# A transformer block on one core: another order of the global attention's pair with three probability buffers, and weights split per stage with finer waits in the layers

## The chip, the cores and the metric

The kernel runs on one core of a Trainium2 chip. The metric is device time in microseconds (us). A core has TensorE (PE in the profile, its weight loads PEld), VectorE (DVE), ScalarE (ACT), GpSimd (POOL) and SyncE (SP), which here only issues DMAs. Each engine runs its own instructions strictly in the order written; they meet through semaphores.

## The reference

The input is four batches of 1024 tokens of 256 numbers. Cut to what matters:

```
h = layernorm(x) * (1 + ca) + sa
q, k, v = tanh(h @ W + b)                      # 16 heads of 64, causal
x = x + ga * tanh(softmax(q k^T / 8) v @ Wo + bo)
h = layernorm(x) * (1 + cb) + sb
for l in range(2):                             # the layers, on h
    q, k, v = shift_token(h) @ wqkv[l]         # 8 heads of 64; norms, scales and rotary on q and k
    h = h + local_attention(q, k, v) @ wo[l]   # own window of 128 and the one before
    a, g = layernorm(shift_token(h)) @ w1[l] + b1[l]
    h = h + (a * gelu(g)) @ w2[l] + b2[l]
x = x + gb * h
```

`shift_token` takes the second half of the features from the token before.

## The kernel before

Matrix products of full precision are made of three: both factors are split into a high part, rounded by a copy or an activation, and a low part, the difference (`three_products`: high by high, high by low, low by high).

**Global attention** (`phase_attention`). Heads are worked in pairs, eight pairs in each of four batches, so 32 rounds of one body that is written out twice (`par` 0 and 1). A pair has twelve units (`UNITS`): a block of 512 queries against 128 keys, the first block with four units on the diagonal (512, 384, 256 and 128 queries), the second with four full ones and four on the diagonal. For a unit PE makes scores (`scores`), ACT the exponential (`probs`), DVE a high copy `p_hi` and a low part `p_lo`, and PE the products with the values (`value_products`, 24 matmuls for a full unit). In the same pair the projections of the next pair are made (`project`, six of them, named in `PROJ`: two for values, then queries and keys). ACT takes each tanh twice, once in full and once rounded, and DVE makes the low part (`split_projection`). The values are transposed by `values`. After units 3 and 11 the sums are divided out (`normalise`, one buffer `ctx_tok`), transposed (`context`) and split (`high_context`, `low_context`). `split_weights` prepares the projection weights of the pair after next. Scores, probabilities and their two parts have two buffers each; a loop over units puts the products of unit u behind the scores of u + 2, and `PROJ_AT`, `VALUES_AT` and `CTX_AT` say at which unit the other steps stand. After eight pairs comes the output projection of the batch.

**Layers** (`phase_layers`). The stream x, 32 tiles of 128 tokens, stays in SBUF. A layer has a body per tile (projection, rotary, local attention, output projection, added to x by DVE's L1314), and then a feed-forward part of eight chunks of four tiles. The weights of both come into one tile `raw` and are split into one pair `w_hi`, `w_lo`: before the first tile for the projection (ACT L998, DVE L1151), and again between the tiles and the chunks for the feed-forward part. SP copies x one token further into `shifted`, batch by batch as the tiles end (L898, L899). DVE waits for all four batches before the statistics of chunk 0 (`chunk_statistics`), then come Pool's power (L946), the normalisation (L1244), PE's transposes (L1432), ACT's and DVE's parts and the projections:

```
                    split_weights(4 * l + 2, F_COLS, 0)
                    hold(dve, s["tick"], (s["shift_in"], 128 * l + 128))
                    chunk_statistics(l, 0, 0, 0)
```

In a tile Pool makes the inverse norms (L936, L937), adds the rotary halves (L941), stages a tile of x (L928) and carries the last token over (L923, L925). In a chunk it adds the bias b2 to x (L974) and makes a power.

Semaphores that DVE, ACT, POOL and PE raise start at 4; `at(n)` adds it. `hold` waits for semaphores and then raises a counter that nobody waits for.

## Time and profile before

| what | value |
|---|---|
| runs | 2948.11 us median of 3 (2948.1 to 2950.08) |
| profiled execution | 2949.01 us, span 2947.2 us |
| busy, share of the span | PE 86%, DVE 70%, ACT 54%, POOL 18% |
| global attention, first scores to the last pair | 111 to 1147 us |
| first projection of layer 0 | 1231 us |
| tiles of layer 0 / chunks of layer 0 | 1262 to 1813 us / 1856 to 2072 us |
| first projection of layer 1 | 2079 us |

The span is what the profiler saw of the program; the profiled execution's time has 1.8 us around it. Busy shares are means over stages with different limits. A line number is one of the code above.

### The profile page before, as it was taken

How to read it: one execution, taken by the hardware profiler on the slowest of the kernel's cores; microseconds unless marked ns; L12 is line 12 of the kernel's file. 1: busy time of each engine (PE TensorE's matmuls, PEld its weight loads, DVE VectorE, ACT ScalarE, POOL GpSimd, SP SyncE). 2: the span in 40 equal slices, each digit the busy share in tenths (PEclk: the TensorE clock that was granted, in tenths of full speed). 3: DMA queues.
4: the chain of work that ended last, by engine and by line, in shares of the span. 5: the costliest groups of instructions: out<-in, count | busy, mean ns of one | idle time of the engine just before them, and what ended most of it. 6: DMA issues, size and time to landing. Idle time of an engine off the chain costs nothing. (4 is left out here: it accounts for less than half of the span.)

```text
span 2947.2 us, 65973 instructions
## 1 busy us (share of the span) xinstructions
PE 2541.4 (86%) x21520; PEld 1928.2 (65%) x21520; DVE 2056.4 (70%) x4571; ACT 1586.2 (54%) x3034; POOL 528.7 (18%) x534
## 2 busy tenths in 40 slices
PE   5699989989998998199999995899799999994996
PEld 3466656666666666177777774788577777773885
DVE  5588778858885885667777774566567777773656
ACT  2577567646764674356656654333466565652332
POOL 0000000000000000333343342111233433431111
PEclk7899999999999999599999998899899999996998
DMA  4400020010002000400000000100100000000003
GB/s 148 154 11 16 6 73 12 15 65 12 16 11 69 11 16 17 146 1 0 7 2 5 4 3 7 45 0 0 34 0 7 0 7 0 7 0 7 0 0 114
DMA packets 74545, 77.25 MB, mean 26 GB/s; under 512 B 4224, under 2 KB 67320, under 8 KB 72952
## 3 DMA queue, kind: packets, MB, share of 16 engines
q1 hardware_dynamic: 74488, 76.46, 7.9%
q8 instruction: 40, 0.66, 0.1%
q14 instruction: 17, 0.14, 0.0%
HBM read 55.48 MB, written 16.78 MB: 25 GB/s over the span
## 5 line engine op out<-in xcount | busy, mean ns | idle before, releaser
L502 ACT ACTIVATE at_p<-at_ps_s,at_shift 128x1024 f32<-128x1024 f32 (+3 forms) x384 | 342.9, 901 | 91.6 <-PE at_ps_s L561 39.9
L434 DVE TENSOR_TENSOR at_p_lo<-at_p,at_p_hi 128x1024 f16<-128x1024 f32 (+3 forms) x384 | 367.9, 958 | 12.1
L1023 ACT ACTIVATE ly_probs<-ly_masked,ly_small,ly_rq 128x256 f32<-128x256 f32 x512 | 302.3, 592 | 63.9 <-DVE ly_small L1206 63.2
L74 PE MATMUL ly_ps<-ly_w_hi,ly_operands 128*128 128x512 f32 (+1 forms) x792 | 293.7, 371 | 15.6 <-DVE ly_operands L1156 9.0
L429 DVE CAST at_p_hi<-at_p 128x1024 f16<-128x1024 f32 (+3 forms) x384 | 213.8, 557 | 94.8 <-PE at_ps_o L575 52.6
L75 PE MATMUL ly_ps<-ly_w_lo,ly_operands 128*128 128x512 f32 (+1 forms) x792 | 273.4, 345 | 0.0
L76 PE MATMUL ly_ps<-ly_w_hi,ly_operands 128*128 128x512 f32 (+1 forms) x792 | 273.1, 345 | 0.0
L573 PE MATMUL at_ps_o<-at_v,at_p_hi 128*128 128x65 f16 x2304 | 248.9, 194 | 24.3 <-DVE at_p_lo L434 24.3
L1409 PEld LDWEIGHTS ly_ps<-ly_values,ly_probs_T 128*128 128x128 f32 x2048 | 258.9, 192 | 15.6 <-issue 0.4
L573 PEld LDWEIGHTS at_ps_o<-at_v,at_p_hi 128*128 128x128 f16 x2304 | 209.9, 96 | 85.1 <-DVE at_p_lo L434 44.3
L1409 PE MATMUL ly_ps<-ly_values,ly_probs_T 128*128 x2048 | 260.1, 270 | 0.0
L574 PE MATMUL at_ps_o<-at_v,at_p_hi 128*128 128x64 f16 x2304 | 247.3, 194 | 0.0
L575 PE MATMUL at_ps_o<-at_v,at_p_lo 128*128 128x65 f16 x2304 | 245.7, 192 | 0.0
L1032 ACT ACTIVATE ly_probs_T<-ly_ps 128x512 f32<-128x512 f32 x256 | 150.3, 587 | 167.1 <-PE ly_ps L1409 150.1
L1389 PE MATMUL ly_ps<-ly_operands_plain 64*128 64x256 f32 x1040 | 183.7, 430 | 50.9 <-DVE ly_small L1203 50.9
L74 PE MATMUL at_ps_m<-at_hT,at_w_hi 128*128 (+1 forms) x396 | 177.0, 447 | 57.2 <-DVE at_v L395 37.2
L1203 DVE CUSTOM_DVE_ANT_0 ly_masked<-ly_ps,ly_mask 128x256 f32<-128x256 f32 x520 | 198.4, 419 | 25.4 <-DVE ly_mask L1303 11.7
L575 PEld LDWEIGHTS at_ps_o<-at_v,at_p_lo 128*128 128x128 f16 x2304 | 213.5, 99 | 0.0
L574 PEld LDWEIGHTS at_ps_o<-at_v,at_p_hi 128*128 128x128 f16 x2304 | 213.1, 97 | 0.4
L1055 ACT ACTIVATE ly_probs<-ly_ps,ly_b 128x512 f32<-128x512 f32 x96 | 66.3, 690 | 256.1 <-PE ly_ps L76 256.1
L471 ACT ACTIVATE at_stage<-at_ps_m,at_bias 128x512 f32<-128x512 f32 x198 | 136.1, 687 | 118.0 <-PE at_ps_m L76 100.4
L905 POOL MEMSET ly_expo<- 128x8 f32 x1 | 0.1, 104 | 1095.3 <-POOLq L331 1095.3
(209 smaller groups left out, 6343.9 us busy)
## 6 DMA issues: line engine op xcount, KB each, us to landing
at_hT<-hT_hi SPq DMA_DIRECT2D x5, 1024.0 KB, 5.2
at_hT<-hT_lo SPq DMA_DIRECT2D x5, 1024.0 KB, 7.7
at_w_raw<-in_Wv SPq DMA_DIRECT2D x34, 128.0 KB, 2.1
at_w_raw<-in_Wq SPq DMA_DIRECT2D x34, 128.0 KB, 2.3
at_w_raw<-in_Wk SPq DMA_DIRECT2D x34, 128.0 KB, 2.3
n_x<-in_states SPq DMA_DIRECT2D x4, 1024.0 KB, 11.6
hT_hi<-n_hi SPq DMA_DIRECT2D x8, 512.0 KB, 3.0
hT_lo<-n_lo SPq DMA_DIRECT2D x8, 512.0 KB, 3.1
```

Of the source, the lines that this page charges most:

```text
L74: pe.matmul(out, w_hi, x_hi, start=first, stop=False, skip_group_check=True)
L75: pe.matmul(out, w_hi, x_lo, start=False, stop=False, skip_group_check=True)
L76: return pe.matmul(out, w_lo, x_hi, start=False, stop=last, skip_group_check=True)
L429: dve.tensor_copy(p_hi[u % 2][:, :, off:], probs[u % 2][:, :, off:]).then_inc(p_hi_done, 1)
L434: dve.tensor_tensor(p_lo[u % 2][:, :, off:], probs[u % 2][:, :, off:], p_hi[u % 2][:, :, off:], ALU.subtract).then_inc(p_lo_done, 1)
L502: step = act.activation(probs[u % 2][:, :, off:], ps_s[u % 2][:, :, off:], ACT.Exp, bias=shift[:], scale=SCORE_SCALE)
L573: pe.matmul(out, ph, ones_hi, start=(kt == 0 and t == 0), stop=False, skip_group_check=True)
L574: pe.matmul(out[:, 0:DH], ph, lo, start=False, stop=False, skip_group_check=True)
L575: step = pe.matmul(out, pl, ones_hi, start=False, stop=(kt == qc * CT + t), skip_group_check=True)
L1023: step = act.activation(pr[:, j % 2, h, :], sm[:, j % 2, h, :], ACT.Exp, bias=small[:, j % 2, 1, h:h + 1], scale=rq[:, par, 2 * j + h:2 * ...
L1203: dve.tensor_tensor_reduce(sm[:, j % 2, h, :], ps_s[h][:, 0:2 * P], mask[:, par].rearrange("p a b -> p (a b)"), 1.0, -3.0e38, ALU.add, ALU ...
L1409: step = pe.matmul(ps_pv[:, cols], pT[:, (2 * slot + h) * P:(2 * slot + h + 1) * P], vv[:, v_slots[slot], cols], start=(j == 0 and h == 0 ...
```

## The change

In the global attention the loop over units and its tables give way to an order written out for PE, ACT and DVE. Probabilities and their parts have three buffers. Values' products, projections and contexts stand at other places; both contexts now come at the end of the pair, and ACT's weight split stands behind tanh 4. In the layers the attention's and the feed-forward part's weights have tiles of their own; the low part lies over the raw weights. The split for the feed-forward part is made by Pool, a piece in each tile, and the split for the next layer's attention by Pool, a piece in each chunk; so are the rotary tables, after the last chunk. Wo is loaded straight to its place. DVE waits for the shifted copy of a batch when it needs it, and SP waits for a batch's copy before it issues the next. In the last layer the preparation for a next one is made too and not used.

```diff
-LAG = 2
...
-PROJ_AT = {1: 0, 2: 1, 6: 2, 7: 3, 9: 4, 10: 5}
-VALUES_AT = {3: 0, 4: 1}
-CTX_AT = 11
...
+P_RING = 3
+NQKV_FREE = (NPJ - 1, NPJ)
...
+        probs = [a.sb(f"at_p{i}", [P, 2, CH]) for i in range(P_RING)]
+        p_hi = [a.sb(f"at_p_hi{i}", [P, 2, CH], F16) for i in range(P_RING)]
+        p_lo = [a.sb(f"at_p_lo{i}", [P, 2, CH], F16) for i in range(P_RING)]
...
+                def high_probs(it, u):
+                    off = unit_offset(u)
+                    dve.wait_ge(exp_done, at(it * NU + u + 1))
+                    dve.wait_ge(pv_done, at(it * NU + u + 1 - P_RING))
...
+                def reciprocals(it, c):
+                    dve.wait_ge(pv_done, at(it * NU + (CT, NU)[c]))
...
+                def normalise(it, c):
+                    n = it * NC + c
                     dve.wait_ge(r_done, at(n + 1))
+                    if c == 1:
+                        dve.wait_ge(ct_mm, n)
...
-                            normalise(it * NC + 1, it * NU + NU)
+                            ahead, dst = NPJ * (it + 1), 1 - par
+                            high_probs(it, 0)
+                            low_probs(it, 0)
+                            high_probs(it, 1)
+                            high_probs(it, 2)
+                            low_probs(it, 1)
+                            low_probs(it, 2)
+                            split_projection(ahead, 0, dst)
+                            split_projection(ahead, 1, dst)
+                            high_probs(it, 3)
+                            low_probs(it, 3)
+                            high_probs(it, 4)
+                            low_values(it + 1, dst)
+                            reciprocals(it, 0)
+                            low_probs(it, 4)
+                            normalise(it, 0)
+                            high_probs(it, 5)
+                            high_probs(it, 6)
+                            low_probs(it, 5)
+                            low_probs(it, 6)
+                            high_probs(it, 7)
+                            low_probs(it, 7)
+                            high_probs(it, 8)
+                            low_probs(it, 8)
+                            split_projection(ahead, 2, dst)
+                            high_probs(it, 9)
+                            high_probs(it, 10)
+                            low_probs(it, 9)
+                            low_probs(it, 10)
+                            high_probs(it, 11)
+                            low_probs(it, 11)
+                            split_projection(ahead, 3, dst)
+                            split_projection(ahead, 4, dst)
+                            reciprocals(it, 1)
+                            normalise(it, 1)
                             split_weights(it + 2)
+                            low_context(it * NC, hp, 0)
+                            split_projection(ahead, 5, dst)
                             low_context(it * NC + 1, hp, 1)
...
@@ -464,11 +497,20 @@
                     hold(act, tick, (ld_w, 48 * n + 48), (pj_mm, at(NPJ * n)))
                     act.activation(w_hi[:], w_raw[:], ACT.Copy).then_inc(wh_done, 1)
...
+                def exps(it, u):
+                    off = unit_offset(u)
+                    act.wait_ge(sc_done, it * NU + u + 1)
+                    act.wait_ge(p_lo_done, at(it * NU + u + 1 - P_RING))
+                    act.activation(probs[u % P_RING][:, :, off:], ps_s[u % 2][:, :, off:], ACT.Exp,
+                                   bias=shift[:], scale=SCORE_SCALE).then_inc(exp_done, 1)
...
+                def tanh_full(base, i, hp):
...
+                def tanh_hi(base, i, hp, dst):
...
+                            ahead, then, dst = NPJ * (it + 1), (hp + 1) % HP, 1 - par
+                            exps(it, 0)
+                            exps(it, 1)
+                            tanh_full(ahead, 0, then)
+                            exps(it, 2)
+                            tanh_hi(ahead, 0, then, dst)
+                            exps(it, 3)
+                            tanh_full(ahead, 1, then)
+                            tanh_hi(ahead, 1, then, dst)
+                            exps(it, 4)
+                            exps(it, 5)
+                            exps(it, 6)
+                            high_values(it + 1, dst)
+                            tanh_full(ahead, 2, then)
+                            tanh_hi(ahead, 2, then, dst)
+                            exps(it, 7)
+                            tanh_full(ahead, 3, then)
+                            exps(it, 8)
+                            exps(it, 9)
+                            tanh_hi(ahead, 3, then, dst)
+                            exps(it, 10)
+                            tanh_full(ahead, 4, then)
+                            exps(it, 11)
+                            tanh_hi(ahead, 4, then, dst)
+                            split_weights(it + 2)
+                            tanh_full(ahead, 5, then)
+                            tanh_hi(ahead, 5, then, dst)
+                            high_context(it * NC, hp, 0)
                             high_context(it * NC + 1, hp, 1)
...
+                            buf = ((it + 1) // HP) % 2
+                            ahead = NPJ * (it + 1)
+                            scores(b, it, par, 1)
+                            project(it, 0, buf)
+                            scores(b, it, par, 2)
+                            scores(b, it, par, 3)
+                            project(it, 1, buf)
+                            value_products(b, it, par, 0)
+                            scores(b, it, par, 4)
+                            scores(b, it, par, 5)
+                            values(0, ahead)
+                            value_products(b, it, par, 1)
+                            values(1, ahead)
+                            value_products(b, it, par, 2)
+                            value_products(b, it, par, 3)
+                            scores(b, it, par, 6)
+                            scores(b, it, par, 7)
+                            project(it, 2, buf)
+                            value_products(b, it, par, 4)
+                            project(it, 3, buf)
+                            scores(b, it, par, 8)
+                            scores(b, it, par, 9)
+                            value_products(b, it, par, 5)
+                            value_products(b, it, par, 6)
+                            scores(b, it, par, 10)
+                            scores(b, it, par, 11)
+                            value_products(b, it, par, 7)
+                            project(it, 4, buf)
+                            value_products(b, it, par, 8)
+                            project(it, 5, buf)
+                            value_products(b, it, par, 9)
+                            value_products(b, it, par, 10)
+                            value_products(b, it, par, 11)
+                            context(it, 0)
+                            scores(b, it + 1, 1 - par, 0)
+                            context(it, 1)
...
-        raw = a.sb("ly_raw", [P, 6144])
-        w_hi = a.sb("ly_w_hi", [P, 4608], F32R)
-        w_lo = a.sb("ly_w_lo", [P, 4608], F32R)
...
+        a_hi = a.sb("ly_a_hi", [P, A_COLS], F32R)
+        f_hi = a.sb("ly_f_hi", [P, F_COLS], F32R)
+        with ExitStack() as shared:
+            a_lo = Allocator(nc, shared).sb("ly_a_lo", [P, A_COLS], F32R)
+        a_raw = a.sb("ly_a_raw", [P, A_COLS])
+        with ExitStack() as shared:
+            f_lo = Allocator(nc, shared).sb("ly_f_lo", [P, F_COLS], F32R)
+        f_raw = a.sb("ly_f_raw", [P, F_COLS])
...
+        SHIFT_TICKS = 32 * (B + 1)
+        A_PIECE, F_PIECE = A_COLS // NCH, F_COLS // NT
...
+                def load_attention(l):
+                    sp.dma_start(a_raw[:].rearrange("p (k n) -> p k n", k=KT),
+                                 io["ffn_wqkv"][l].rearrange("(k p) n -> p k n", p=P)).then_inc(s["ld_attn"], 16)
+                    sp.dma_start(rope[:].rearrange("p a t d -> p (a t d)"), io["rope"]).then_inc(s["ld_attn"], 16)
+                    sp.dma_start(rows[:], io["qk_rows"][l].partition_broadcast(P)).then_inc(s["ld_attn"], 16)
+                load_attention(0)
                 with sp.Fori(0, L) as l:
 
...
                     hold(sp, s["tick"], (s["ya_done"], at(NCH * l)))
-                    hold(sp, s["tick"], (s["w_lo_done"], at(4 * l + 2)))
-                    hold(sp, s["tick"], (s["rope_q"], at(4 * l + 4)))
-                    hold(sp, s["tick"], (s["wo_copied"], at(l + 1)))
-                    sp.dma_start(raw[:, 0:KT * 2 * HT * P].rearrange("p (k n) -> p k n", k=KT),
+                    sp.dma_start(wo, io["ffn_wo"][l].rearrange("(k p) n -> p k n", p=P)).then_inc(s["ld_wo"], 16)
+                    sp.dma_start(f_raw[:, 0:KT * 2 * HT * P].rearrange("p (k n) -> p k n", k=KT),
...
+                    for b in range(B):
 
                         hold(sp, s["tick"], (s["xa_done"], at(l * NT + b * TB + TB)))
-                        sp.dma_start(shifted[1:P, ds(b * TB, TB), :], x[0:P - 1, ds(b * TB, TB), P:D]).then_inc(s["shift_in"], 16)
-                        sp.dma_start(shifted[0:1, ds(b * TB + 1, TB - 1), :],
-                                     x[P - 1:P, ds(b * TB, TB - 1), P:D]).then_inc(s["shift_in"], 16)
+                        if b:
+                            hold(sp, s["tick"], (s["shift_in"], SHIFT_TICKS * l + 32 * b))
+                        sp.dma_start(shifted[1:P, b * TB:(b + 1) * TB, :], x[0:P - 1, b * TB:(b + 1) * TB, P:D]).then_inc(s["shift_in"], 16)
+                        sp.dma_start(shifted[0:1, b * TB + 1:(b + 1) * TB, :],
+                                     x[P - 1:P, b * TB:(b + 1) * TB - 1, P:D]).then_inc(s["shift_in"], 16)
+                    hold(sp, s["tick"], (s["shift_in"], SHIFT_TICKS * l + 32 * B))
+                    sp.sem_inc(s["shift_in"], 32)
+                    hold(sp, s["tick"], (s["qkv_mm"], at(3 * (NT + 2) * (l + 1))))
+                    hold(sp, s["tick"], (s["ra_done"], at(6 * (NT + 1) * (l + 1))))
+                    load_attention((l + 1) % L)
...
+                def split_ffn_weights(l, t):
+                    cols = ds(t * F_PIECE, F_PIECE)
+                    hold(pool, s["tick"], (s["ld_ffn"], 80 * l + 80))
+                    pool.tensor_copy(f_hi[:, cols], f_raw[:, cols]).then_inc(s["fw_hi"], 1)
+                    hold(pool, s["tick"], (s["fw_hi"], at(nth(l, t) + 1)))
+                    pool.tensor_tensor(f_lo[:, cols], f_raw[:, cols], f32(f_hi[:, cols]), ALU.subtract).then_inc(s["fw_done"], 1)
...
+                    cols = ds(c * A_PIECE, A_PIECE)
+                    hold(pool, s["tick"], (s["ld_attn"], 48 * l + 96))
...
+                            split_ffn_weights(l, t)
...
                         inverse_deviation(l, c + 1)
+                        split_attention_weights(l, c)
+                    for i in range(4):
+                        pool.tensor_tensor(rope[:, i], rope[:, i], rows[:, i, :].unsqueeze(1).broadcast_to([P, TB, DH]),
+                                           ALU.mult).then_inc(s["rope_next"], 1)
...
+                act.wait_ge(s["ld_attn"], 48)
+                for i in range(2):
+                    part = slice(i * A_COLS // 2, (i + 1) * A_COLS // 2)
+                    act.activation(a_hi[:, part], a_raw[:, part], ACT.Copy).then_inc(s["w_hi_done"], 1)
...
-                    split_weights(0, "ld_attn", 64 * l + 64, QKV_COLS)
...
-                    split_weights(1, "ld_ffn", 80 * l + 80, F_COLS)
+                    hold(act, s["tick"], (s["ld_ffn"], 80 * l + 80))
...
+                dve.wait_ge(s["ld_attn"], 48)
+                for i in range(4):
+                    dve.tensor_tensor(rope[:, i], rope[:, i], rows[:, i, :].unsqueeze(1).broadcast_to([P, TB, DH]),
+                                      ALU.mult).then_inc(s["rope_q"], 1)
+                for i in range(2):
+                    part = slice(i * A_COLS // 2, (i + 1) * A_COLS // 2)
+                    after(dve, "w_hi_done", i + 1)
+                    dve.tensor_tensor(a_lo[:, part], a_raw[:, part], f32(a_hi[:, part]), ALU.subtract).then_inc(s["w_lo_done"], 1)
+                after(dve, "rope_q", 4)
...
-                    split_weights(4 * l, QKV_COLS, 0)
-                    split_weights(4 * l, QKV_COLS, 1)
                     stream_lo(l, 0, 0)
-                    dve.tensor_copy(wo, raw[:, QKV_COLS:A_COLS].rearrange("p (k n) -> p k n", k=LP)).then_inc(s["wo_copied"], 1)
...
+                    after(dve, "rope_next", 4 * l)
...
-                    split_weights(4 * l + 2, F_COLS, 0)
-                    hold(dve, s["tick"], (s["shift_in"], 128 * l + 128))
+                    hold(dve, s["tick"], (s["shift_in"], SHIFT_TICKS * l + 32))
                     chunk_statistics(l, 0, 0, 0)
                     chunk_statistics(l, 0, 1, 0)
                     chunk_normalise(l, 0, 0)
-                    split_weights(4 * l + 2, F_COLS, 1)
                     chunk_lo(l, 0, 0)
+                    after(dve, "fw_done", NT * (l + 1))
...
+                            if par == 1:
+                                hold(dve, s["tick"], (s["shift_in"], SHIFT_TICKS * l + 32 * (cc + 2)))
                             chunk_statistics(l, c + 1, 0, nxt)
...
+                after(pe, "w_lo_done", 2)
...
-                    after(pe, "w_lo_done", 4 * l + 2)
+                    after(pe, "aw_done", NCH * l)
...
-                    after(pe, "wo_copied", l + 1)
+                    hold(pe, s["tick"], (s["ld_wo"], 16 * l + 16))
...
-                    hold(pe, s["tick"], (s["w_lo_done"], at(4 * l + 4)))
+                    hold(pe, s["tick"], (s["fw_done"], at(NT * (l + 1))))
```

## Rows read from the trace of the kernel before

**Rows 1.** The page, part 1: busy us (share of the span) and instructions.
```profile
PE 2541.4 (86%) x21520; PEld 1928.2 (65%) x21520; DVE 2056.4 (70%) x4571; ACT 1586.2 (54%) x3034; POOL 528.7 (18%) x534
```

**Rows 2.** Windows: length, busy us (instructions) of each engine, clock, DMA share, GB/s.
```profile
528.45:557.96 29.51, 27.16 (x367) 18.43 (x366) 25.62 (x38) 20.84 (x29) 0.00 (x0) 1.00 0.05 13
...
1262.00:1810.00 548.00, 522.19 (x3320) 406.79 (x3319) 394.24 (x1192) 328.63 (x860) 206.54 (x225) 0.99 0.01 3
1856.00:2072.00 216.00, 212.44 (x1216) 185.77 (x1216) 127.64 (x295) 79.37 (x128) 24.86 (x15) 0.99 0.03 11
```

**Rows 3.** Timeline of ACT, one pair to the next: start, duration, instruction.
```profile
524.03 0.83 ACT L465 ACTIVATE at_w_hi<-at_w_raw 128x768 fp32r<-128x768 f32 x1
...
553.44 0.85 ACT L465 ACTIVATE at_w_hi<-at_w_raw 128x768 fp32r<-128x768 f32 x1
```

**Rows 4.** Timeline of PE in that pair; in brackets the idle time before and its releaser.
```profile
539.43 0.50 PE L74 MATMUL at_ps_m<-at_hT,at_w_hi 128*128 x1 [1.16 <-DVE at_v L395]
...
541.76 0.39 PE L557 MATMUL at_ps_s<-at_q1hi,at_k1hi 64*128 64x512 f16 x2
...
542.52 0.50 PE L74 MATMUL at_ps_m<-at_hT,at_w_hi 128*128 x1
...
550.06 0.47 PE L74 MATMUL at_ps_m<-at_hT,at_w_hi 128*128 x1
...
551.53 0.20 PE L573 MATMUL at_ps_o<-at_v,at_p_hi 128*128 128x65 f16 x1
...
552.38 0.23 PE L557 MATMUL at_ps_s<-at_q1hi,at_k1hi 64*128 64x128 f16 x2
...
552.77 0.61 PE L581 MATMUL at_ps_m<-ident,at_ctx_tok 128*128 128x128 f32 x4
```

**Rows 5.** Timeline of DVE in that pair.
```profile
541.94 0.69 DVE L429 CAST at_p_hi<-at_p 128x1024 f16<-128x1024 f32 x1
542.67 1.22 DVE L434 TENSOR_TENSOR at_p_lo<-at_p,at_p_hi 128x1024 f16<-128x1024 f32 x1
543.81 0.69 DVE L390 TENSOR_TENSOR at_q0lo<-at_stage,at_q0hi 128x512 f16<-128x512 f32 x1
```

**Rows 6.** Timelines of five engines, from the last tile to the first chunk of layer 0.
```profile
1812.67 0.42 DVE L1314 TENSOR_TENSOR stream<-stream,ly_ps 128x256 f32 x1
...
1812.94 4.14 ACT L998 ACTIVATE ly_w_hi<-ly_raw 128x2304 fp32r<-128x2304 f32 x2 [3.20 <-PE ly_ps L1422]
...
1814.43 24.74 SPq L899 DMA_DIRECT2D ly_shifted<-stream  x1
...
1814.71 1.64 POOL L937 TENSOR_TENSOR ly_rq<-ly_norm,ly_expo 128x8 f32<-128x8 f32 x1
...
1843.18 0.29 DVE L1225 BATCH_NORM_STATS2 ly_st<-stream 128x6 f32<-128x128 f32 x1 [25.53 <-DMA ly_shifted<-stream]
...
1849.41 1.96 PE L1432 MATMUL ly_ps<-ident,ly_sq 128*128 128x128 f32 x8 [37.12 <-DVE ly_sq L1244]
1855.82 0.79 PE L74 MATMUL ly_ps<-ly_operands,ly_w_hi 128*128 128x512 f32 x1 [4.45 <-DVE ly_operands L1251]
```

**Rows 7.** Timelines of DVE and PE, and a window, at the start of layer 1.
```profile
2075.50 3.43 DVE L1151 TENSOR_TENSOR ly_w_lo<-ly_raw,ly_w_hi 128x1536 fp32r<-128x1536 f32 x2 [2.33 <-ACT ly_w_hi L998]
...
2079.39 0.80 PE L74 MATMUL ly_ps<-ly_w_hi,ly_operands 128*128 128x512 f32 x1 [5.07 <-DVE ly_operands L1156]
...
2076.00:2080.00 4.00, 0.61 (x2) 0.52 (x3) 4.00 (x6) 0.51 (x3) 0.50 (x2) 0.58 0.00 0
```

**Rows 8.** Timelines of DVE and Pool in chunk 1.
```profile
1899.30 1.95 DVE L1262 TENSOR_TENSOR ly_operands<-ly_rope_t,ly_operands 128x512 fp32r<-128x512 f32 x1
...
1904.38 0.68 DVE L1262 TENSOR_TENSOR ly_operands<-ly_rope_t,ly_operands 128x512 fp32r<-128x512 f32 x1
...
1898.32 2.39 POOL L974 TENSOR_TENSOR stream<-stream,ly_b 128x1024 f32 x1 [3.30 <-DVE ly_sq L1244]
```

**Rows 9.** Timeline of Pool in a tile.
```profile
1518.27 0.19 POOL L925 CAST ly_carry<-ly_operands 128x2 f32 x1 [5.62 <-DVE ly_operands L1156]
```

203 lines of the change are left out of this document (66 added, 137 removed).

## The prediction

> **What bounds the kernel now.** I read the page first, for the shares of the engines [rows 1]: PE is busy 86% of the span, so time can be won only where PE stands still. Then the windows by stage [rows 2]. Three stages matter: the global attention (32 pairs of heads), the local attention of two layers (64 tiles), and their feed-forward parts (16 chunks). In the feed-forward window PE is busy 212.44 of 216 us: nothing to win there. In the local attention it is 522.19 of 548. In one pair of the global attention it is 27.16 of 29.51 us, by ends that are modelled and so hide part of each gap. The distance of two equal ACT instructions gives the pair's period, 29.41 us here [rows 3] and 29.5 by the window's ends [rows 2]; I use 29.47. Last I read the timelines of the places where PE stands: 37.12 us at the entry of a feed-forward part [rows 6], and a few at the start of layer 1 [rows 7]. The chain that ended last reaches only the last 27 us of work and was of no use.
>
> **Part 1, the pair's order.** What PE must do in a pair, start to start [rows 4]: a score unit of 512 queries off the diagonal takes 0.76 (541.76 to 542.52), one of 128 on the diagonal 0.39 (552.38 to 552.77); the two between by their width 0.53 and 0.67, and one of 512 on the diagonal 0.1 more than off it: 4 x 0.76 + 2 x 2.45 = 7.9. A projection takes 1.47 (550.06 to 551.53), six 8.8. A value product of 24 matmuls takes 0.85 (551.53 to 552.38), so 216 of them 7.65. Four groups of transposes are 0.45 each by their starts (the 0.61 of the row of 552.77 less the tail of its last), 1.8. Sum 26.2 us. So PE's queue stands some 3.3 of 29.47 us. The largest single wait is 1.16, for DVE's copy of the low values, ahead of projection 2 [rows 4].
>
> DVE's sum: 38 instructions, 25.62 us busy [rows 2]. Neighbours overlap by 0.08 (a low part of 1.22 is followed after 1.14), but a high part with its low part next costs 0.73 where 0.69 less the overlap would be 0.61 [rows 5]. 25.62 - 38 x 0.08 + 0.9 for those is 23.5. ACT is lower, 20.84. So PE stays the longest queue; the question is which waits stay. I walked the new written order once through a pair, each engine in its order, with these costs and 0.1 per handover:
> - Before, two buffers tie a high part to the value product two units back. With three it is the product three back, and no high part waits over 0.1 in the walk.
> - The low values are there at 11.7 us of the walk and PE reaches projection 2 at 12.8: the 1.16 goes.
> - At the pair's end PE runs context 0, the next pair's score 0, context 1. DVE's second normalisation (0.2 + 0.6) lies beneath the first two (0.45 + 0.86). The next projection 0 now waits for low context 0, which stands behind the weight split: about 0.25 us, the only wait that stays.
> - ACT's weight split now waits for projection 5, with two tanh, both contexts and the next pair's exp 0 behind it: six instructions at the row's mean of 20.84 / 29 = 0.72, 4.3 us [rows 2]. PE has 1.3 of products, then 0.45 + 0.86 + 0.45 + 0.67 and 1.47 + 0.53 before it needs that exp, 5.7. Without this cover a pair would lose the 4.3.
>
> The walk gives 26.6; I take 26.8 for what a walk by means misses. 32 x (29.47 - 26.8) = 85 us. Each batch's output projection now waits for low context 0, 0.8 after context 1: 4 x 0.8 = 3. Net -82. Ends: 26.3 (the sum) gives -98, 28.1 (half of the waits stay) -41.
>
> **Part 2, entry of the feed-forward part** [rows 6]. DVE's last addition starts at 1812.67; then DVE waits until 1843.18 for the shifted copy of the *last* batch, whose issue alone holds SP 24.74 us. Statistics, norm and transposes bring PE's first transpose at 1849.41 and its first projection at 1855.82. The new wait asks for batch 0's copy, issued 24 tiles of 17 us earlier (548 us for 32 tiles in rows 2). So the statistics start at 1813.2, 30.0 earlier. Pool's power for them now stands behind its last inverse norm, 1814.71 + 1.64 = 1816.35, where it would be asked for at about 1815.9: 0.5 lost. The weight splits that go (4.14 on ACT, and DVE's half of it) stood beside the wait and are worth 0; had they stayed, ACT's would end at 1817.1, still ahead of the transposes at 1819. Net -29.5 a layer, -59. The last batch's copy is needed by chunk 6, over 150 us later. Ends: -61, and -50 if a new wait of 5 appears.
>
> **Part 3, start of a layer** [rows 7]. In layer 1 DVE starts splitting the projection weights at 2075.50, for 3.43, and PE projects from 2079.39. With the split gone there remain Pool's staging, two transposes and the copies of the operand by ACT and DVE, which can start at once: PE at about 2075.5, -3.9. The granted clock was 0.58 there, mostly the lower of its two levels (1.2 GHz), after a nearly idle PE; if the shorter pause keeps it high, 2 more. I take -4.5 (ends -3, -6). In layer 0 the four table products (0.69 each, as 512 columns in rows 5) move ahead of PE's start and two waits shrink: +1 (ends 0, +4). The loads of Wo, W1 and W2, six issues on SP's queue, lie under the first tiles: 0.
>
> **Part 4, splits on Pool.** Pool adds 1024 columns in 2.39 us [rows 8], 2.3 ns a column. A tile's piece of 144 columns is two instructions of 0.35; Pool idles 5.62 us before its next job [rows 9], which hides them. A chunk's piece is two of 384 columns, 0.9 each, after a power. What counts is DVE: a subtraction of 512 columns took 1.95 where its like take 0.68 while Pool's addition ran, and ended with it [rows 8]. In a tile DVE is busy 394.24 of 548 [rows 2] and PE fills the time: 0. In a chunk up to 1.4 us of DVE's work comes late; DVE is busy 127.64 of 216 there, so most is taken up: 0.3 x 16 = +5. Ends: 0, and 64 x 0.7 + 16 x 1.4 = +67 if nothing is covered. SP loads the next layer's weights only behind the shifts, from about 1841; Pool waits for them in chunk 0 until about 1854 and is back before chunk 1 asks for its power, near 1863. Pool's four table products (1.2 each) end before chunk 7 does: 0.
>
> The Trainium skill (SBUF — State Buffer, Who interferes with whom) says that a DVE instruction with two SBUF inputs, or in a two-port mode, and a GpSimd instruction exclude each other for the whole instruction. The 1.95 beside 2.39 [rows 8] agrees; by that rule each new Pool piece can hold DVE for its full length, which is rival 3.
>
> **Sum.** -82 - 59 - 4.5 + 1 + 5 = -139.5. The profiled execution took 2949.01, 0.9 above the runs' median of 2948.11: 2809.5, on the runs' scale 2808.6. I forecast 2809.
>
> **Rivals.**
> 1. *Half of the pair's waits stay* (period 28.1). For it: DVE's 23.5 and PE's 26.2 are both near the period, and three ordered queues wait for each other. Against: no long wait in the walk. -41 in place of -82: 2850.
> 2. *The entry keeps half of its wait under another name*, Pool's last weight pieces or ACT's. Against: Pool idles a third of a tile of 17 us [rows 9]. 2809 + 30 = 2839.
> 3. *Pool holds DVE*, +67 in place of +5: 2871. Against: DVE's idle share in both stages.
> 4. *Slower:* ACT's chain at the pair's end is uncovered. PE would have to wait 6.3 us a pair (32.5 against 26.2): 32 x 3 = 97 on top of the period before, against the layers' -57.5, gives 2988. It turns slower from a period of 31.3 on. The chain is 4.3 and its cover 5.7, so it would have to start more than 6 us late.
> 5. *The new order changes nothing in the pair* (29.47): 2891.
>
> **Chances.** Forecast (2785 to 2830) 0.60; rival 1 0.18; 2 0.07; 3 0.07; 5 0.03; 4 0.04; within 0.2% of before 0.01. The range holds the forecast and rivals 1 and 2: 2782 to 2860. Under 0.2% (6 us) this measurement can't tell a difference from none. Faster 0.95, same 0.01, slower 0.04.
>
> **What would show it.** ACT's weight splits 26.8 apart; no PE wait over 0.5 ahead of projection 2. PE's idle time at each entry about 7 instead of 37 us, and no DVE wait on the shifted copies. Tiles still 17 us, chunks 27. The prediction is wrong if PE waits for ACT or DVE between the pair's scores, if DVE's subtractions of 512 columns grow in the chunks, or if PE's granted clock falls in the attention.

## The result and the profile after

The changed kernel takes 2810.18 us (median of 4 runs, 2808.05 to 2811.05), the kernel before 2948.11 (2947.35 to 2950.08): a ratio of 0.953, 95% interval 0.9514 to 0.9547. The forecast was 2809. So the total is right to 1 us, but not each term: two large ones are off by 15 and 11 us in opposite directions, and the runs below were made to price them.

The page's first part after the change (engine, busy us, share of the span, instructions), against [rows 1]:

```profile
span 2805.9 us, 66485 instructions
...
PE 2517.2 (90%) x21520; PEld 1920.9 (68%) x21520; DVE 2038.4 (73%) x4559; ACT 1559.1 (56%) x3028; POOL 607.2 (22%) x702
```

PE has the same 21520 matmuls and is busy 90% of the span, where it was 86%.

**Stage by stage.** Both spans, cut at the same instructions of both traces (starts, us). "Forecast" is the prediction's own terms put into these stretches.

| stretch, from the end of the one above | before | after | change | forecast |
|---|---|---|---|---|
| start to PE's last output transpose for `at_ps_s` | 1165.9 | 1069.0 | -96.9 | -82 |
| to ACT's first squares of layer 0 | 70.8 | 74.7 | +3.9 | +1 |
| to DVE's last addition of the tiles | 575.9 | 575.7 | -0.2 | 0 |
| to DVE's addition of chunk 0 | 73.0 | 42.3 | -30.7 | -29.2 |
| to its addition of chunk 7 | 186.3 | 193.5 | +7.2 | +2.1 |
| to the first squares of layer 1 | 12.6 | 10.5 | -2.1 | -4.5 |
| to the last addition of its tiles | 575.5 | 575.8 | +0.3 | 0 |
| to its addition of chunk 7 | 258.8 | 236.1 | -22.7 | -27.1 |
| to the end | 28.3 | 28.3 | 0 | 0 |

The row before the last holds an entry of -30.1 and, from chunk 0 to chunk 7, +7.3, as layer 0 has -30.7 and +7.2.

**The pair.** ACT's weight split (L498 now; start, us, engine, line), against [rows 3]:

```profile
511.20 0.84 ACT L498 ACTIVATE at_w_hi<-at_w_raw 128x768 fp32r<-128x768 f32 x1 [0.56 <-PE at_ps_m L76]
...
537.65 0.84 ACT L498 ACTIVATE at_w_hi<-at_w_raw 128x768 fp32r<-128x768 f32 x1 [0.55 <-PE at_ps_m L76]
```

The period is 26.45 us. The window of just this pair (length, then busy time and instructions of each engine, granted clock, DMA share), against the first row of [rows 2]:

```profile
core 0: us, PE busy (x) PEld busy (x) DVE busy (x) ACT busy (x) POOL busy (x), PEclk, DMA share, GB/s
...
511.20:537.65 26.45, 26.31 (x370) 18.21 (x367) 24.70 (x39) 20.31 (x29) 0.00 (x0) 1.00 0.05 15
```

PE is busy 26.31 of 26.45 us. And PE's waits from 300 to 1000 us of the changed kernel (who waited for whom, us in total, times, longest):

```profile
PE at_ps_s L636 <- issue: 9.5, 3, 3.4
PE at_ps_o L679 <- DVE at_y L481: 3.9, 3, 1.3
PE at_ps_s L74 <- DVE at_cT_lo L423: 2.4, 3, 0.8
```

All three come three times in 700 us: they belong to the ends of batches. Inside a pair there is no wait of PE left that the view lists. The 1.16 us for the low values [rows 4] is gone.

**The entry of the feed-forward part**, against [rows 6]. DVE's last tile addition and its next instructions, then PE's first projection:

```profile
1719.48 0.42 DVE L1414 TENSOR_TENSOR stream<-stream,ly_ps 128x256 f32 x1
1720.12 0.29 DVE L1331 BATCH_NORM_STATS2 ly_st<-stream 128x6 f32<-128x128 f32 x1 [0.23 <-issue]
...
1733.06 0.79 PE L74 MATMUL ly_ps<-ly_operands,ly_f_hi 128*128 128x512 f32 x1 [4.45 <-DVE ly_operands L1357]
```

From DVE's last addition to PE's first projection it was 1855.82 - 1812.67 = 43.15 us; it is 1733.06 - 1719.48 = 13.58: 29.6 less. DVE no longer waits for a shifted copy. The entry of layer 1 shows the same 29.6. The stretch to DVE's addition of chunk 0 is shorter by another 1.1 us in layer 0 and 0.5 in layer 1, and that goes with the clock. The windows of the first 6.2 us of projections in layer 0, before and after:

```profile
1855.80:1862.00 6.20, 6.18 (x15) 4.93 (x16) 0.00 (x0) 0.50 (x1) 0.00 (x0) 0.53 1.01 397
```

```profile
1733.00:1739.20 6.20, 6.14 (x20) 4.96 (x21) 0.56 (x1) 0.69 (x1) 0.00 (x0) 0.73 0.08 19
```

After a pause of 37 us PE did 15 matmuls there at a granted clock of 0.53 (its lower level, 1.2 GHz, nearly all the time), after one of 7.5 it does 20 at 0.73. At layer 1 the same windows have 17 matmuls at 0.59 and 19 at 0.69.

**The last chunk of a layer**, where the forecast had nothing. Pool's last piece of the weights (L1044, L1046) and its four table products (L1080):

```profile
1931.43 1.02 POOL L1030 TENSOR_TENSOR ly_nrm<-ly_nrm,ly_expo 128x4 f32<-128x4 f32 x1 [19.11 <-DVE ly_nrm L1340]
1932.41 0.51 POOL L1044 CAST ly_a_hi<-ly_a_raw  x1
1933.10 1.23 POOL L1046 TENSOR_TENSOR ly_a_lo<-ly_a_raw,ly_a_hi  x1 [0.18 <-POOL ly_a_hi L1044]
1934.30 4.97 POOL L1080 TENSOR_TENSOR ly_rope<-ly_rope,ly_rows 128x512 f32<-128x512 f32 x4
```

DVE in the same microseconds, and PE, which waits for it:

```profile
1933.38 0.97 DVE L1345 SCALAR_TENSOR_TENSOR ly_nrm<-ly_mv,ly_nrm 128x4 f32<-128x4 f32 x1
1934.39 1.27 DVE L1350 TENSOR_SCALAR ly_sq<-stream,ly_nrm 128x128 f32 x1
1935.58 1.32 DVE L1350 TENSOR_SCALAR ly_sq<-ly_shifted,ly_nrm 128x128 f32 x1
1936.82 1.30 DVE L1350 TENSOR_SCALAR ly_sq<-stream,ly_nrm 128x128 f32 x1
1938.05 1.30 DVE L1350 TENSOR_SCALAR ly_sq<-ly_shifted,ly_nrm 128x128 f32 x1
1939.27 0.34 DVE L1350 TENSOR_SCALAR ly_sq<-stream,ly_nrm 128x128 f32 x1
...
1940.50 1.36 PE L1533 MATMUL ly_ps<-ident,ly_sq 128*128 128x128 f32 x8 [3.89 <-DVE ly_sq L1350]
```

While Pool works, four normalisations of DVE take 1.3 us each; as soon as Pool has ended (1939.27) they take 0.34. Their starts are 1.19 to 1.24 apart, about one product of Pool (4.97 / 4) each: the two engines take turns. From chunk 6's addition to chunk 7's it is 32.2 us, where two chunks earlier it was 26.8: the last chunk costs 5.4 us more, in both layers. PE waits 3.89 us, and the window from 1935 to 1945 shows what that does to its clock (columns as above):

```profile
1935.00:1945.00 10.00, 6.11 (x30) 5.18 (x29) 6.63 (x10) 1.21 (x2) 4.26 (x4) 0.83 0.00 0
```

A granted clock of 0.83, where the chunks before it (1765 to 1925) have 1.00: after its pause PE stood for a part of the window at the lower of its two levels (1.2 GHz).

**The start of layer 0.** DVE makes the table products and the low weights, PE waits for the second, ACT loads a table:

```profile
1119.80 4.84 DVE L1226 TENSOR_TENSOR stream<-stream,modB 128x2048 f32<-128x2048 f32 x1 [1.90 <-ACT stream L1093]
1124.56 7.18 DVE L1251 TENSOR_TENSOR ly_rope<-ly_rope,ly_rows 128x512 f32<-128x512 f32 x4
1131.67 3.41 DVE L1256 TENSOR_TENSOR ly_a_lo<-ly_a_raw,ly_a_hi 128x1536 fp32r<-128x1536 f32 x2
...
1135.62 0.68 PE L1461 MATMUL ly_ps<-ident,ly_xs 128*128 128x128 f32 x2 [58.45 <-DVE ly_a_lo L1256]
...
1136.58 1.28 ACT L1107 ACT_TABLE_LOAD   x1 [14.06 <-PE ly_ps L1461]
...
1138.89 0.79 PE L74 MATMUL ly_ps<-ly_a_hi,ly_operands 128*128 128x512 f32 x1 [2.59 <-DVE ly_operands L1262]
```

PE's wait for `w_lo_done` now stands ahead of the first transposes, which don't need the low weights; and the first activation of ACT's loop is now the copy of the operand, so that the table load sits between PE's transposes and PE's projection. At layer 1 the same load shows again at 1957.95.

The four table products take 7.18 us where the forecast had 4 x 0.69. The times of a single one (ns, shortest/median/longest), and what Pool did beside the longest:

```profile
L1251 DVE TENSOR_TENSOR ly_rope<-ly_rope,ly_rows x4: 677/880/4976, 1124.6 to 1130.9; 128x512 f32<-128x512 f32 x4
```

```profile
1124.72 4.87 POOL L998 TENSOR_TENSOR stream<-stream,modB 128x2048 f32<-128x2048 f32 x1 [2.23 <-DVE stream L1226]
```

One product of DVE lasted as long as an addition of Pool that is in both kernels. Before the change the same addition stood beside DVE's split of the low weights, whose two instructions took 7.71 us together, against 3.41 now. So this price is not new; it has only moved from the split to the products.

### The profile page after: what moved, and what is told of

Same layout as the page of the kernel before. It is cut to its first block and busy times, and to the rows that moved or that the text cites. A ratio compares the mean times of both kernels' runs of the same rounds, so it can differ in the third digit from the quotient of the medians.

```text
span 2805.9 us, 66485 instructions
## 1 busy us (share of the span) xinstructions
PE 2517.2 (90%) x21520; PEld 1920.9 (68%) x21520; DVE 2038.4 (73%) x4559; ACT 1559.1 (56%) x3028; POOL 607.2 (22%) x702
## 5 line engine op out<-in xcount | busy, mean ns | idle before, releaser
L504 ACT ACTIVATE at_p<-at_ps_s,at_shift 128x1024 f32<-128x1024 f32 (+3 forms) x384 | 335.9, 900 | 84.6 <-PE at_ps_s L636 44.9
L405 DVE TENSOR_TENSOR at_p_lo<-at_p,at_p_hi 128x1024 f16<-128x1024 f32 (+3 forms) x384 | 357.2, 951 | 5.5
L400 DVE CAST at_p_hi<-at_p 128x1024 f16<-128x1024 f32 (+3 forms) x384 | 206.1, 556 | 50.0 <-PE at_ps_o L662 24.8
L660 PE MATMUL at_ps_o<-at_v,at_p_hi 128*128 128x65 f16 x2304 | 237.7, 193 | 0.5 <-DVE at_p_lo L405 0.5
L661 PE MATMUL at_ps_o<-at_v,at_p_hi 128*128 128x64 f16 x2304 | 236.9, 194 | 0.0
L662 PE MATMUL at_ps_o<-at_v,at_p_lo 128*128 128x65 f16 x2304 | 235.8, 192 | 0.0
L660 PEld LDWEIGHTS at_ps_o<-at_v,at_p_hi 128*128 128x128 f16 x2304 | 210.7, 96 | 35.3 <-issue 26.6
L1025 POOL TENSOR_TENSOR ly_rope_a<-ly_rope_a,ly_rope_t 128x512 f32<-128x512 f32 x132 | 175.9, 1333 | 76.0 <-DVE ly_rope_t L1283 76.0
L74 PE MATMUL ly_ps<-ly_a_hi,ly_operands 128*128 128x512 f32 x408 | 183.3, 449 | 7.8 <-DVE ly_operands L1262 7.8
L1020 POOL TENSOR_TENSOR ly_rk<-ly_norm,ly_expo 128x8 f32<-128x8 f32 x68 | 112.2, 1650 | 272.1 <-DVE ly_norm L1271 272.1
```

The source lines that it names most:

```text
L74: pe.matmul(out, w_hi, x_hi, start=first, stop=False, skip_group_check=True)
L400: dve.tensor_copy(p_hi[u % P_RING][:, :, off:], probs[u % P_RING][:, :, off:]).then_inc(p_hi_done, 1)
L405: dve.tensor_tensor(p_lo[u % P_RING][:, :, off:], probs[u % P_RING][:, :, off:], p_hi[u % P_RING][:, :, off:], ALU.subtract).then_inc(p_lo ...
L504: act.activation(probs[u % P_RING][:, :, off:], ps_s[u % 2][:, :, off:], ACT.Exp, bias=shift[:], scale=SCORE_SCALE).then_inc(exp_done, 1)
L660: pe.matmul(out, ph, ones_hi, start=(kt == 0 and t == 0), stop=False, skip_group_check=True)
L661: pe.matmul(out[:, 0:DH], ph, lo, start=False, stop=False, skip_group_check=True)
```

## Experiments

Each was timed against the kernel before on the same chip; ratios are to it, with their 95% interval. Differences to the changed kernel are to its 2810.18 us, which was measured in another session. The kernel before read 2946.99 to 2948.95 in these sessions, and the runs of one kernel lie some 3 us around their median, so such a difference is good to about 2 us. Where the parts are smaller, the stretches of the traces are given.

### The two halves of the change by themselves

Attention alone is the changed `phase_attention` with the old layers; layers alone is the old `phase_attention` with the changed layers.

> The changed global attention (order and three buffers) with the layers of the kernel before. Theory: the attention's part is worth more than the -82 of the prediction; by the first row of the last output transposes of both traces, 1173.8 against 1076.9 us, it is -97, so 2948 - 97 = 2851 us (2847 to 2855), with equal splits of ACT 26.45 apart instead of 29.41. Rival: the attention gives the -82 of the prediction and the other 15 us come from somewhere behind it that only shows in the whole kernel: 2866.

Measured: 2851.01 us (ratio 0.9669, 0.9653 to 0.9685). It is 98 less than before, as the theory said, with splits 26.45 apart.

> The changed layers with the global attention of the kernel before. Theory: the layers are worth 13 us less than the -57.5 of the prediction; by the traces, from the last output transposes to the end 1773.4 against 1729.0 us, they give -44: 2904 us (2900 to 2908). Rival: the layers' terms were right and the two parts cost each other something: 2890.5.

Measured: 2912.54 us (0.9875, 0.9858 to 0.9891): -36, less than either expected. The halves add up to -134 of the -138 of the whole. The trace shows where the layers alone lose against the same layers in the full change: the tiles of a layer, from DVE's first addition to its last, take 532.9 us instead of 530.6. The windows of the tiles, first of the changed kernel, then of this one:

```profile
1189.00:1719.00 530.00, 504.81 (x3220) 393.24 (x3218) 385.32 (x1162) 317.74 (x831) 226.19 (x279) 1.00 0.01 3
```

```profile
1285.60:1818.20 532.60, 505.31 (x3220) 393.16 (x3218) 388.89 (x1163) 319.47 (x831) 226.23 (x279) 1.00 0.01 3
```

The instructions are the same; every second tile takes 17.13 us instead of 16.98, and DVE's busy time is 3.6 longer. What settles the one rhythm or the other I have not found. The tiles of the two layers give 4.8 us of the 8.5 that are missing, and the stretch from the last chunk to the end, untouched by any edit, 2.9 more: it takes 31.2 us in the profiled execution of this run and of three later ones, and 28.2 to 28.3 in the others. So a difference of a few us between two kernels whose layers are equal need not have a cause in the edit.

### Order or buffers

Both on the old layers. Two buffers under the new order is one constant:

```diff
-P_RING = 3
+P_RING = 2
```

> The new written order of the pair, with two probability buffers in place of three; layers of the kernel before. Theory: the new order needs the third buffer, since DVE makes the high part of unit u + 1 ahead of the low part of u and with two buffers that high part waits for the value product two units back, which PE has put later than before; each such wait then holds the low part behind it and PE's next product. The period is no shorter than the old 29.47, so 2948 or more (up to 3010). Rival: the order alone does it and the buffers hardly matter: a period of 26.5 to 27.3, 2852 to 2880.

Measured: 3097.13 us (1.0494, 1.0477 to 1.0512), 148 more than before. The splits are 549.79 - 515.61 = 34.18 us apart; 32 x (34.18 - 29.41) = 153. DVE's waits from 300 to 1000 us, and one of them in the timeline:

```profile
DVE at_p_hi L400 <- PE at_ps_o L662: 156.7, 124, 5.0
...
513.34 0.43 DVE L400 CAST at_p_hi<-at_p 128x512 f16<-128x512 f32 x1 [2.75 <-PE at_ps_o L662]
```

Three buffers under the old order:

```diff
-                                act.wait_ge(p_lo_done, at(it * NU + u - 1))
+                                act.wait_ge(p_lo_done, at(it * NU + u - 2))
...
-                                dve.wait_ge(pv_done, at(it * NU + u - 1))
+                                dve.wait_ge(pv_done, at(it * NU + u - 2))
```

and `u % 3` for the probabilities and their parts.

> The old order of the pair with three probability buffers, and waits three units back; layers of the kernel before. Theory: in the old order PE comes to each product before its low part is there because projections, values and splits stand between the units at unlucky places, and a third buffer lets ACT and DVE start no earlier, since the scores still have two buffers. A gain of at most 0.6 us a pair: 2929 to 2950. Rival: the buffers are what gives the gain, and the order little: 2855 to 2880.

Measured: 2948.77 us (0.9999, 0.999 to 1.0009): nothing. PE's waits from 300 to 1000 us:

```profile
PE at_ps_m L74 <- DVE at_v L395: 24.4, 21, 1.2
PE at_ps_m L581 <- DVE at_ctx_tok L402: 12.2, 20, 0.6
```

The wait for the low values, 1.2 us a pair, is what it was [rows 4]: it hangs on the place of `low_values`, not on a buffer. In the kernel before the same view had 15.2 us of waits for `at_p_lo` and 2.0 for `at_ctx_tok`; the third buffer took the first down to 5.5, and the second grew by 10.

So the gain belongs to neither part: the buffers alone give 0, the order alone costs 148, both give 98.

The last question here was whether DVE's own new order matters, in which the high part of unit u + 1 stands ahead of the low part of u. The edit, for the units 1, 5 and 9:

```diff
                             high_probs(it, 1)
-                            high_probs(it, 2)
                             low_probs(it, 1)
+                            high_probs(it, 2)
                             low_probs(it, 2)
```

> The new order of the pair and three buffers (layers of the kernel before), but DVE makes the low part of units 1, 5 and 9 ahead of the high part of the next unit, as the old order did. Theory: PE has the slack for it, since its products of a unit now stand two or more steps behind; a pair costs at most 0.3 us more: 2851 to 2861. Rival: DVE's changed order is what lets PE run through, and without it half of the gain goes: 2880 to 2900.

Measured: 2854.50 us (0.9682, 0.9667 to 0.9697) against 2851.01 with the look-ahead; the splits are 538.47 - 512.01 = 26.46 apart, so in a pair it is worth nothing, and the intervals overlap. What is left of the 3.5 us lies in the length of a batch, 242.9 us against 242.2; two runs further down that keep the look-ahead (the later table products, and everything together) show 242.8 as well, so it is not the look-ahead's.

> The same with two buffers. Theory: the high part of unit u waits for the product of u - 2, which PE's new order puts behind the scores of u and u + 1, whatever DVE's own order: still slower than before, 3000 to 3100. Rival: it was DVE's look-ahead (the high part of u + 1 ahead of the low part of u) that held the two-buffer kernel back, and without it the time is 2851 to 2950.

Measured, in two executions: 2988.83 us (1.0141, 1.0122 to 1.0159), a period of 541.43 - 510.82 = 30.61. The time lies between the two expectations. It is 42 us above the kernel before, so DVE's look-ahead made up 106 of the 148 us that the two-buffer kernel lost; the rest comes with the other engines' new order, which wants the third buffer with either order of DVE (DVE waits for value products 94.0 us from 300 to 1000 us, against 156.7).

### The entry

```diff
-                    hold(dve, s["tick"], (s["shift_in"], SHIFT_TICKS * l + 32))
+                    hold(dve, s["tick"], (s["shift_in"], SHIFT_TICKS * l + 32 * B))
```

> The changed kernel, but DVE waits for the shifted copies of all four batches before the statistics of chunk 0, as before. Theory: this wait is the whole of the entry's gain. The copies are now issued one after the other by SP, the last after the last tile, so DVE waits again some 30 us at each of two entries: 2810 + 59 = 2869 us (2860 to 2872). Rival: the separate weight tiles and Pool's splits give a part of it, or the paced copies land sooner, and the wait costs half: 2840.

Measured: 2869.03 us (0.9733, 0.9717 to 0.975), 58.9 more than the changed kernel. DVE stands after its last addition as it did before:

```profile
1718.03 0.42 DVE L1414 TENSOR_TENSOR stream<-stream,ly_ps 128x256 f32 x1
1748.39 0.29 DVE L1331 BATCH_NORM_STATS2 ly_st<-stream 128x6 f32<-128x128 f32 x1 [29.94 <-SPq L981]
```

The entry of layer 0 takes 72.6 us up to the addition of chunk 0, against 73.0 before and 42.3 with the early wait. So without the early wait the separate weight tiles and Pool's splits are worth next to nothing. The run doesn't show the reverse, that the early wait alone would give the whole gain. In the kernel before, DVE's first half of the weight split stood between its last tile addition and the statistics:

```profile
1815.10 2.56 DVE L1151 TENSOR_TENSOR ly_w_lo<-ly_raw,ly_w_hi 128x2304 fp32r<-128x2304 f32 x1 [2.00 <-ACT ly_w_hi L998]
```

It ends 4.99 us after the start of the last addition (1812.67), and in the changed kernel the statistics start 0.64 after it. By these rows, an estimate, the early wait with the old splits in their old places would have lost some 4 us of the 30 at each entry. No run tests that.

### Pool beside DVE

The table products, moved behind DVE's last normalisation:

```diff
+                    after(pool, "xnd", nth_norm(l, NCH) + 1)
                     for i in range(4):
                         pool.tensor_tensor(rope[:, i], rope[:, i], rows[:, i, :].unsqueeze(1).broadcast_to([P, TB, DH]),
```

> The changed kernel; Pool makes the four rotary table products only after DVE has made the last chunk's normalisation (a wait on it in front of them). Theory: these products hold DVE's eight normalisations of the last chunk (1.3 us each in place of 0.34) and PE waits 3.9 us for them and runs at the lower clock behind it, in both layers: DVE back to 0.34, PE's wait gone, about 5 us a layer, 2800 us (2798 to 2803). Rival: it is the split piece just ahead of them (DVE's short instruction takes 0.87 instead of 0.16 in every chunk) or another cause, and nothing or up to 2 us comes back: 2808 to 2810.

Measured: 2799.94 us (0.9491, 0.9475 to 0.9507), 10.2 less than the changed kernel. The products now run where DVE has time, and the normalisation is back to 0.34:

```profile
1939.08 0.34 DVE L1351 TENSOR_SCALAR ly_sq<-stream,ly_nrm 128x128 f32 x1
1939.34 0.34 DVE L1351 TENSOR_SCALAR ly_sq<-ly_shifted,ly_nrm 128x128 f32 x1
...
1939.76 5.48 POOL L1081 TENSOR_TENSOR ly_rope<-ly_rope,ly_rows 128x512 f32<-128x512 f32 x4 [2.28 <-DVE ly_sq L1351]
```

From chunk 0 to chunk 7 of layer 0 it takes 188.0 us instead of 193.5, and in layer 1 188.1 instead of 193.6: 11 us by the traces.

Then the pieces of the weights in each chunk. First without most of their work: a copy in place of the high part and the subtraction, so that the kernel leaves out the split and layer 1 works with weights that have no high and low part.

> The changed kernel; in each chunk Pool only copies its piece of the attention's weights in place, and leaves out the high part and the subtraction (layer 1 works with unsplit weights), 0.5 us of Pool instead of 1.7. Theory: the pieces lie in DVE's slack; DVE's short instruction of 0.87 goes back to 0.16, but the distance of Pool's additions stays at 26.2 us, and the time within 3 us of 2810. Rival: Pool's pieces cost PE a few tenths a chunk as the prediction had it, 16 x 0.3: 2805.

Measured: 2801.69 us (0.9502, 0.9486 to 0.9518), 8.5 less by the medians, 5.0 by the spans of the two profiled executions. Pool's additions are 26.63 apart, as before the change. The theory (the pieces cost nothing) was wrong and the rival right in kind: seen from chunk to chunk the pieces cost 0.25 us each. The rest of the gain is in the last chunk (31.3 us instead of 32.2), whose table products begin sooner.

Then the same pieces whole, but behind DVE's next normalisation; the table products come later with the last piece:

```diff
-                    hold(pool, s["tick"], (s["ld_attn"], 48 * l + 96))
+                    hold(pool, s["tick"], (s["ld_attn"], 48 * l + 96), (s["xnd"], at(nth_norm(l, c) + 2)))
```

> The changed kernel, only with the wait for DVE's next normalisation in front of Pool's piece in each chunk (the table products behind the last piece come later with it). Theory: distance of Pool's additions 26.62 in place of 26.88, about 4 us, and about 6 a layer of the table products: 2794 us (2791 to 2798). Rival: the additions stay 26.88 apart, since Pool's two-operand pieces now hold DVE's subtractions instead: 2798 to 2800.

Measured: 2795.07 us (0.9485, 0.947 to 0.9499), 15.1 less than the changed kernel. Pool in one chunk:

```profile
1851.94 0.50 POOL L1044 CAST ly_a_hi<-ly_a_raw  x1 [3.27 <-DVE ly_sq L1350]
1852.63 1.01 POOL L1046 TENSOR_TENSOR ly_a_lo<-ly_a_raw,ly_a_hi  x1 [0.18 <-POOL ly_a_hi L1044]
1853.59 2.85 POOL L1075 TENSOR_TENSOR stream<-stream,ly_b 128x1024 f32 x1
...
1880.21 2.86 POOL L1075 TENSOR_TENSOR stream<-stream,ly_b 128x1024 f32 x1
```

The additions are 26.62 apart, and from chunk 0 to chunk 7 it takes 186.3 us, the time of the kernel before; so it does in layer 1. With this one wait Pool's splits and products in the chunks cost nothing. A subtraction of DVE still stretches (1.21 at 1879.59 for its usual 0.68), but there PE doesn't wait for it.

### The layer's start, and everything together

```diff
                 with act.Fori(0, L) as l:
+                    act.activation(warm2[:], ident[:, 0:1], ACT.Copy)
                     after(act, "y_mm", HT * NCH * l)
...
-                after(pe, "w_lo_done", 2)
                 with pe.Fori(0, L) as l:
                     after(pe, "ya_done", NCH * l)
                     stream_T(l, 0, 0)
+                    after(pe, "w_lo_done", 2)
                     after(pe, "aw_done", NCH * l)
```

and DVE's low weights ahead of its table products. The three moves were timed together, not one by one.

> The changed kernel with three small moves at a layer's start: PE transposes the first tile before it waits for the low weights, DVE makes the low weights ahead of the table products in layer 0, and ACT runs a one-column copy at the head of its loop, so that its table load of 1.28 us comes before it waits for PE. Theory: in layer 0 the first projection comes about 3.4 us earlier (transposes and load no longer behind DVE's two jobs) and in layer 1 1.3 us earlier: 2805.5 us (2804 to 2807). Rival: the first projection in layer 0 waits for DVE's low weights and products anyhow, only the load's 1.3 us a layer comes back: 2807.5.

Measured: 2805.74 us (0.9519, 0.9503 to 0.9534), 4.4 less than the changed kernel. The load lies where ACT idles, the transposes are ready early, and PE projects at 1135.30 instead of 1138.89 (0.65 of it since DVE's last addition began sooner too):

```profile
1121.88 1.28 ACT L1166 ACT_TABLE_LOAD   x1
...
1132.02 0.68 PE L1463 MATMUL ly_ps<-ident,ly_xs 128*128 128x128 f32 x2 [54.92 <-POOL ly_xs L1013]
...
1135.30 0.79 PE L74 MATMUL ly_ps<-ly_a_hi,ly_operands 128*128 128x512 f32 x1 [2.60 <-DVE ly_operands L1264]
```

> The changed kernel with the three moves at a layer's start, and with Pool's piece of the attention's weights in each chunk, and with it the table products, behind a wait for DVE's next normalisation. Theory: the three gains add: start 3.4 + 1.3, table products about 6 a layer, pieces 0.26 a chunk of 16 (the distance of Pool's additions back from 26.88 to 26.62): 2810 - 5 - 12 - 4 = 2789 us (2786 to 2793). Rival: the later piece only moves the collision to another DVE instruction and costs the same 0.26 a chunk: 2793.

Measured: 2792.35 us (0.9472, 0.9459 to 0.9485), 17.8 less than the changed kernel. The sum of the two parts measured singly would be 15.1 + 4.4 = 19.5. Against the later pieces alone (2795.07, on the same chip) the intervals overlap; that the layers' starts add to them is seen in the traces, where the stretches to the first squares take 71.4 and 8.6 us instead of 74.3 and 10.7.

## Why the prediction was right, and which steps were not

- **The pair: right mechanism, too small.** The walk gave 26.6 and I took 26.8 "for what a walk by means misses"; the period is 26.45. 32 x (29.47 - 26.45) = 96.6 in place of 85. The batch ends were priced at +3. PE does wait 0.8 there for the low context, but on balance they cost nothing: from one batch's output transposes to the next it is 242.1 us instead of 266.4, and eight pairs account for 24.2 of the 24.3. So the term of -82 measured -97 (trace) and -98 (attention alone), next to the end of -98 that the sum of PE's own work gave. The walk was off by 0.15 a pair and the allowance on top of it by another 0.2, upwards, where nothing in the walk asked for it. PE's own sum of 26.2 was nearer than the value taken. (The range's end of 26.3 is called that sum; 26.2 would give -102.) Of the two parts, the prediction credited the buffers with taking the high part's wait away and the order with the rest; the runs show neither gives anything alone.
- **The entry: right, with one part not shown.** -29.5 a layer, measured -29.6 to the first projection in both layers, and 58.9 for both by undoing the one wait. Behind the shorter pause PE's clock was higher, 1.1 us in layer 0 and 0.5 in layer 1, which I had allowed for only at the start of layer 1. The splits that left ACT and DVE are worth 0 only beside the long wait; once it is gone, DVE's half of 2.56 us would stand ahead of the statistics, some 4 us a layer by the estimate above. The prediction looked only at ACT's half there. The total is untouched, since they did leave.
- **The chunk's pieces on Pool: right.** +0.3 a chunk forecast, 0.26 measured (26.62 to 26.88). The tiles' pieces: 0 forecast, 0.3 us or less a layer measured. The prediction says of the subtraction in [rows 8] that it ended with Pool's addition; by the rows it ended at 1901.25, 0.54 after the addition's 1900.71. It named as a sign of being wrong that these subtractions grow, and they did: 14 of the 96 took 2.0 us before, 12 take 2.6 now and 14 take 0.9, 9 us of DVE's time in all. It cost PE little, since only those 0.26 us a chunk came through.
- **The table products at 0: wrong, the step that failed.** "Pool's four table products end before chunk 7 does: 0" asked only whether the products were done in time for their own reader. It did not ask what DVE does at that moment, although [rows 8] had shown what Pool's two-operand work does to DVE: the normalisation, on which PE waits. The stretches put it at 193.5 - 186.3 - 7 x 0.26 = 5.4 us in layer 0 and 5.5 in layer 1; moving it gave back 10.2 in all by the medians, 11 by the traces.
- **The layer's starts: too hopeful.** Layer 0 was +3.9, not +1. The forecast counted the four products but missed that PE's wait had moved ahead of its transposes, and that the first activation in ACT's loop, and so the table load of 1.28 us, was now a different one. In layer 1 it is -2.1 instead of -4.5. The forecast had the copies of the operand start at once behind the transposes, but the load still stands in that chain: before the change it came ahead of ACT's split, for which DVE's split waited, and now it comes ahead of ACT's copy. Moving it gave back 0.9 us in layer 1 by the traces; where the rest of the 2.4 went is not shown.
- **The sum.** By the stretches: attention -96.9, layer 0's start +3.9, entries with chunk 0 -30.7 and -30.1, the other chunks 14 x 0.26 = +3.6, table products +10.9, layer 1's start -2.1, tiles +0.1, together the -141.3 of the two spans, against -139.5 (the medians of the runs are 137.9 apart). The attention gave 15 us more than forecast and the entries 2, the table products took 11 and the starts 5; they cancelled by luck. A total that is right to 1 us here says nothing on the terms.
- **The rivals.** Half of the pair's waits staying, half of the entry's, and an uncovered chain of ACT are excluded by the waits shown above, and a pair that doesn't change (rival 5) by its period. Rival 3, Pool holding DVE, was true in kind: its own pieces cost 4 of its 67 us, and the table products, which it did not count, 11.

The 1.3 us of DVE's normalisation has one SBUF tensor as input and a column of scalars. The Trainium skill (SBUF — State Buffer, Who interferes with whom) says that such an operation can enter a two-port mode, if its operands meet some conditions, and then contends with GpSimd, that whoever issues first has the shared ports for the whole instruction and the other is blocked entirely. The trace agrees, with four instructions of 1.3 in turn with products of 1.24.

## What to carry to other kernels

- When work is moved to an idle engine, don't only ask whether it is done in time: look at what DVE does in just those microseconds when the work goes to Pool, and whether the bound engine waits for that. Here one wait that moved the work by 5 us was worth 10 us, and the engine was idle both ways.
- A buffer and an order can each be worthless alone. Test them in both combinations before crediting either, and where an order leaves the bound engine no wait, forecast close to the sum of its own work (here 26.2 for a measured 26.45).
- Undoing one part of a change shows that the part is needed, not that it is enough. Here the early wait was undone and cost everything, but the early wait without the moved splits was never run.
- After moving an instruction out of a loop's head, look for what stood behind it unseen: a table load, or a wait that is now asked for too early.

## What was not expected of the hardware

- DVE and Pool took turns: an instruction of DVE of 0.34 us ended 1.2 us after the one before, four times in a row, while Pool's products of 512 columns ran back to back; a DVE product of 512 columns lasted 4.98 beside an addition of Pool of 4.87, 0.68 without it; a DVE instruction on four columns took 0.97 beside Pool's subtraction, 0.15 without it (before the change).
- Equal instructions in the tiles settled into either of two rhythms, 16.98 or 17.13 us for every second tile, which makes 2.3 us a layer. The stretch behind the last chunk, the same in every kernel here, took either 28.2 or 31.2.
